# The state's products moved from behind the scores to ahead of the outputs, as two tiles instead of four

## What is computed

```python
A = jnp.einsum('bhntd,bhnsd->bhnts', q, k)
A = A * jnp.where(mask, jnp.exp(jnp.where(mask, dec, 0.0)), 0.0)
o_intra = jnp.einsum('bhnts,bhnsd->bhntd', A, v)
...
o_int = jnp.einsum('bhtd,bhde->bhte', qc * jnp.exp(gcc)[..., None], S)
kd = kc * jnp.exp(gtc[..., None] - gcc)[..., None]
S = jnp.exp(gtc)[..., None, None] * S + jnp.einsum('bhtd,bhte->bhde', kd, vc)
```

## Time and profile before

| | us |
|---|---|
| median of 3 runs | 402.62 (401.43 to 403.20) |
| the profiled execution | 398.42 |
| its span, first to last instruction | 396.7 |
| PE busy | 372.7 (94%) |
| DVE busy | 306.7 (77%) |
| ACT busy | 289.2 (73%) |
| POOL busy | 279.7 (71%) |

### The profile page before, as it was taken

How to read it: one execution, slowest core, us unless ns; L and a number is a source line. 1 busy time by engine, 2 the same in 40 slices (tenths; PEclk the granted TensorE clock), 3 DMA queues, 4 the chain that set the end, 5 groups by cost and what they waited for, 6 DMA issues and landing times.

```text
span 396.7 us, 14345 instructions
## 1 busy us (share of the span) xinstructions
PE 372.7 (94%) x4077; PEld 318.2 (80%) x4078; DVE 306.7 (77%) x859; ACT 289.2 (73%) x889; POOL 279.7 (71%) x245
## 2 busy tenths in 40 slices
PE   7997799999999999999999998999999999999990
PEld 6665577777777787787787877899999999999990
DVE  4988798999888889888888889567767767677750
ACT  3888887888788887878787885566667666666660
POOL 8002553687788877888788863388888888888883
PEclk9996999999999999999999999999999999999996
DMA  8944579457465545566564522254545455455530
GB/s 232 247 136 151 198 244 325 138 169 193 158 202 148 152 132 161 162 197 179 167 190 118 167 65 67 44 70 65 72 64 68 62 70 68 59 74 67 61 32 0
DMA packets 59097, 51.31 MB, mean 129 GB/s; under 512 B 7200, under 2 KB 51392, under 8 KB 59072
## 3 DMA queue, kind: packets, MB, share of 16 engines
q1 hardware_dynamic: 45936, 42.07, 37.6%
q0 software_dynamic: 12272, 8.54, 15.4%
q10 hardware_dynamic: 864, 0.40, 0.4%
HBM read 33.14 MB, written 18.30 MB: 130 GB/s over the span
## 4 chain that ended last, share of the span: by engine, by line
PE 63%; ACT 13%; DVE 9%; issue 7%; DMA 3%; POOL 2%; ACTq 1%; DVEq 1%; SPq 0%; POOLq 0%
PE psA L977 16%; PE psVG L965 16%; PE psVG L771 11%; PE psT L859 7%; ACT sq L1157 3%; DVE ms L1470 3%; ACT v_sb L1139 3%; ACT E L1148 3%; ACT th L1130 2%; PE psO L825 2%; PE psKS L814 2%; DMA x_all<-in_L_attn_x_dram 2%; DVE kd L1514 2%; PE psA L648 1%; PE psKS L956 1%
## 5 line engine op out<-in xcount | busy, mean ns | idle before, releaser
L620 POOL DMA_INDIRECT out_dram<-yw,sidx x71 | 114.8, 1618 | 29.4 <-DVE yw L1685 9.0
L1148 ACT ACTIVATE E<-gcB,ngc 128x128 f32<-128x128 f32 x256 | 78.4, 404 | 0.9 <-DMA gcB<-decay_rows 0.9
L577 POOL DMA_INDIRECT sorted_rows<-x_all,pos_i x64 | 63.8, 998 | 13.5 <-issue 9.2
L561 POOL TENSOR_TENSOR rms<-msn,neg_half 128x8 f32<-128x8 f32 x32 | 54.3, 1697 | 24.2 <-DVE msn L1474 23.8
L554 POOL TENSOR_SCALAR_AFFINE_SELECT E<-E 128x1024 f32<-128x1024 f32 x32 | 35.1, 1095 | 42.9 <-ACT E L1148 30.8
L1130 ACT ACTIVATE th<-psVG,x_all 128x256 f32<-128x256 f32 x64 | 26.8, 470 | 31.7 <-PE psVG L771 31.7
L825 PEld LDWEIGHTS psO<-v_sb,pr 128*64 128x64 f32 x1024 | 33.3, 141 | 13.8 <-issue 13.5
L825 PE MATMUL psO<-v_sb,pr 128*64 128x64 f32 x1024 | 37.7, 228 | 3.0 <-DVE pr L1503 3.0
L977 PE MATMUL psA<-xT_all,v_sb 128*128 x288 | 38.4, 277 | 0.4 <-DVE yb L1683 0.4
L965 PE MATMUL psVG<-xgT,gcB 128*128 128x128 f32 x288 | 38.6, 278 | 0.0
L977 PE MATMUL psA<-xT_all,th 128*128 x280 | 37.9, 279 | 0.5 <-issue 0.2
(11 more groups left out here) (210 smaller groups left out, 948.0 us busy)
## 6 DMA issues: line engine op xcount, KB each, us to landing
gcB<-decay_rows SPq DMA_DIRECT2D x32, 512.0 KB, 4.9
sorted_rows<-blank SPq DMA_DIRECT2D x12, 396.0 KB, 5.7
xg<-sorted_rows SPq DMA_DIRECT2D x71, 66.0 KB
x_all<-in_L_attn_x_dram SPq DMA_DIRECT2D x16, 256.0 KB, 5.2
out_dram<-res SPq DMA_DIRECT2D x32, 128.0 KB, 2.0
eqB<-decay_exp_rows SPq DMA_DIRECT2D x32, 64.0 KB
w1b<-in_L_ffn_w_dram SPq DMA_DIRECT2D x8, 256.0 KB
xT_all<-in_L_ffn_w_dram SPq DMA_DIRECT2D x32, 64.0 KB
```

Source lines behind the costliest of these rows:

```text
L561: nc.gpsimd.tensor_tensor(rms[:], msn[:], neg_half[:, 0:2 * H], ALU.pow).then_inc(rms_ready, 1)
L577: nc.gpsimd.indirect_dma_start(out=sorted_dram, out_offset=bass.IndirectOffsetOnAxis(ap=pos_i[:, t:t + 1], axis=0), in_=x_all[:, t, :], in ...
L620: nc.gpsimd.indirect_dma_start(out=out_rows, out_offset=bass.IndirectOffsetOnAxis(ap=sidx[j][:], axis=0), in_=yw[j][:], in_offset=None, bo ...
L1148: last = nc.scalar.activation(E[j][:, k, h * P:(h + 1) * P], gcB[j][:, k * H + h, :], ACT.Exp, bias=ngcf[:, bass.ds((s * 2 + k) * H + h, 1)])
```

## The change

`state` makes two products instead of four: for each pair of heads all 64 key columns by the 128 value columns of both heads. So it computes the blocks of head a's keys by head b's values as well; the copy's mask, which now takes 128 columns of psKS twice instead of 64 four times, sets them to zero as it did with the repeated ones. Each product is a tile of 64 output partitions, as in the outputs. In `step` the call moves from behind `scores` to behind `proj_vg`, directly ahead of `outputs`. The waits of `state` (kd_ready, v_copied) move with it. The calls outside `step` (sequences 0, 1 and 31) keep their place and take the new form.

```diff
                 pe.wait_ge(kd_ready, s + 1)
                 pe.wait_ge(v_copied, s + 1)
-                for h in range(H):
-                    last = nc.tensor.matmul(psKS[h * DK:(h + 1) * DK, HV:HV + DV], kd[:, h * DK:(h + 1) * DK], v_sb[j][:, 0, h * DV:(h + 1) * DV],
-                                            start=True, stop=True)
+                for c in range(2):
+                    last = nc.tensor.matmul(psKS[c * 2 * DK:(c + 1) * 2 * DK, HV:HV + 2 * DV], kd[:, c * 2 * DK:(c + 1) * 2 * DK],
+                                            v_sb[j][:, 0, c * 2 * DV:(c + 1) * 2 * DV], start=True, stop=True)
                 last.then_inc(s_ready, 1)
...
                 first_keys(i, j)
                 proj_qk(*turn(i, j, 1, 2))
                 scores(i, j)
-                state(i, j)
                 project_out(*turn(i, j, -2, 2))
                 if extra:
                     extra()
                 proj_vg(*turn(i, j, 1, 2))
                 if behind_vg:
                     behind_vg()
+                state(i, j)
                 outputs(i, j)
                 transpose_on(*turn(i, j, -1, 2))
...
-                nc.vector.tensor_tensor(S_sb[:].rearrange("p (h d) -> p h d", d=DV), bc(psKS[:, HV:HV + DV].unsqueeze(1), [P, H, DV]),
-                                        headmask[:].rearrange("p (h d) -> p h d", d=DV), ALU.mult).then_inc(s_copied, 1)
+                nc.vector.tensor_tensor(S_sb[:].rearrange("p (c n) -> p c n", c=2), bc(psKS[:, HV:HV + 2 * DV].unsqueeze(1), [P, 2, 2 * DV]),
+                                        headmask[:].rearrange("p (c n) -> p c n", c=2), ALU.mult).then_inc(s_copied, 1)
```

## The result

The changed kernel takes 403.0 us in the median of 21 runs (401.7 to 405.3), the kernel before 401.4 in 21 runs beside it (399.5 to 403.6): a ratio of 1.0036, 95% interval 1.0022 to 1.005, which is 0.9 to 2.0 us; the medians differ by 1.6. The change is slower by less than the 0.5% that the prediction took as its line. The forecast, 404.7, stands 1.7 too high, and its own range, 403.4 to 406.0, begins 0.4 above the measured time: 1.2 of the 1.7 is the base (402.6 was the median of three runs, 401.4 that of 21), 0.5 the sum (+2.1 for +1.6).

The account below looks back on a forecast made before the run. A ring from outputs through square, sum, kd, state, project_out and proj_vg bounds the lap. 0.22 inserted less 0.15 slack gives +0.07 over 20 laps, plus 0.7 elsewhere: +2.1 on 402.6, so 404.7 us, range 403.4 to 406.0.

Parts of the forecast that it names:

- The ring through square, sum and kd: Outputs, square, sum, kd, state, project_out, proj_vg, outputs: this ring sets the lap at 6.45, against PE's own 6.32.
- The state's new form, +0.22: State's two rounds of 0.11, ahead of the outputs, lengthen the ring by 0.22; bounds 0.11 to 0.44.
- the first rival: PE's own order bounds the lap, with one mode-change drain gone: laps of 6.29, 399.2 us; chance 0.12.
- The slack at proj_vg, 0.15: proj_vg, released by the probabilities, can come 0.15 earlier, not 0.38: lag 0.23 now, 0.08 then.
- Laps of 6.44 and 6.45: Lap lengths of the attention loop in the earlier trace, forecast to become 6.52, +0.07 each.
- The steps outside: Steps outside the 20 laps from 98 to 227 us: step 2 gains 0.3, others lose, together +0.7 us.
- The sum: Whole kernel: 20 laps of 0.07 plus 0.7 for the other steps, +2.1 us.
- PE's order as the bound: Square or probabilities have slack, so PE's own length sets laps of 6.29: 399.2 us; chance 0.12.
- Cheap state: State's rounds cost only 0.11 in the new place, laps 0.04 shorter: 401.9 us; chance 0.12.
- Late copy: DVE's state copy ends over 0.25 later than put, or the mode drains once more: 407.4 us; chance 0.09.
- Serial tiles: State's two tiles run one after the other, insertion 0.44, 0.22 more per step: 410.6 us; chance 0.05.

Follow-up runs that it names:

- form: Kernel before with the new two 64-column state products at the old place behind the scores: 402.8 us, ratio 1.0056 to the kernel before.
- after_look1: The changed kernel, unchanged, in a third traced execution: span 403.9 us.
- before_kd_first: Kernel before with DVE's kd (decay_k) put ahead of the sum of squares: 406.2 us, ratio 1.012 to the kernel before.
- place: Changed kernel with the old four 32-column state products at the new place ahead of the outputs: 407.6 us, ratio 1.0151 to the kernel before.
- before_two: Kernel before with two scatters in every step and the 14 left all in step 29: 414.1 us, ratio 1.0267 to the kernel before.
- after_two: Changed kernel with two scatters in every step and the 14 left all in step 29: 415.5 us, ratio 1.0295 to the kernel before.
- before_gap: Kernel before with a GpSimd fill between the two back-to-back scatters of three-scatter steps: 407.1 us, ratio 1.0097 to the kernel before.
- after_gap: Changed kernel with a GpSimd fill between the two back-to-back scatters of three-scatter steps: 406.5 us, ratio 1.0084 to the kernel before.

## Why the prediction came out as it did

*What bounds a lap.* Right for undisturbed laps. The ring through square, sum and kd is shown by form, and in the changed kernel it closes through the probabilities: PE's waits name them, and no wait for kd is left.

*The state's new form, +0.22.* Right to the hundredth between state and outputs. From proj_vg to the outputs' end it is 3.40 (131.81 to 135.21) for 3.16: +0.24, since the state starts 0.02 later behind proj_vg than the own halves did.

The step on which the first rival rested was the drain at a change of tiling. The last score is 0.21 ahead of project_out in the changed kernel (130.53 to 130.74), as it was ahead of the state in the earlier trace rows; behind proj_vg one change is left as before, and state and own halves, of one tiling, have none between them. From the state to what follows it is 0.27 in the same tiling (own halves, changed kernel) and 0.37 across a change of it (project_out, form): 0.10 for the change, if nothing else sets the two apart, which no run tells. That PE time was saved, and it didn't count, as PE's own length is not the bound. By the Trainium skill (TensorEngine Tiling (Array Packing), Key Properties) PE drains on a change of the mode and not of the tile alone; the two figures agree with that.

*The slack at proj_vg, 0.15.* This is the step of the prediction that failed: the mechanism was right, and the term was mis-sized. It was 0.23 - 0.08: a mean of 0.21 and 0.25, read from sums of rounded rows (0.22 and 0.25 unrounded in that trace), less a lag to which I had added the time from the load to its product. Measured, from the pair with two scatters a step: proj_vg starts 0.25 and 0.26 behind the probabilities in the old kernel's two kinds of lap, and 0.055 behind them in both of the changed one. Slack 0.20. The probabilities also end 0.01 to 0.02 sooner behind the outputs, since the square takes 0.60 where it took 0.61 to 0.62. 0.235 - 0.20 - 0.02 = +0.017, as the laps say. 20 x 0.07 = 1.4 should have been 20 x 0.017 = 0.3.

*Laps of 6.44 and 6.45.* Here the prediction rested on a row that was true and not typical. In the other traces half of the laps are 6.73 to 6.82, in both kernels, and in these the change costs nothing that can be seen, as the scatters set them. In the four typical traces before and three after, proj_vg 11 to 31 is 132.7 (132.5 to 133.1) and 133.1 (133.0 to 133.4): +0.4, of which 0.15 is the last lap.

*The steps outside.* Step 2 gained 0.3 as forecast (lap 2 is 8.32 for 8.64). Laps 3 to 5 lose 0.13, 0.14 and 0.24, forecast +0.5. Laps 6 to 8 were to lose 0.1 and lose 0.56, all of it in lap 7, which holds the first late signal: 7.64 for 6.85 to 7.25 before. With two scatters a step lap 7 is 6.59 for 6.61, so it is how the disturbance falls, not the change's own length. Lap 9 loses 0.0 for 0.1. From proj_vg 2 to 11 that is +0.76 in the typical traces (64.3 to 65.1), +0.27 in the pair of two. The forecast's own sum for these steps doesn't fit its text: it has a term of 0.2 where the text gives 3 x 0.03 for steps 6 to 8, and with the text's terms it is +0.6, not +0.7.

*The sum.* From step 2 on the typical traces give 0.76 + 0.42 - 0.29 (behind proj_vg 31) = +0.9, where +1.6 (0.9 to 2.0) is measured; without after_look1, whose part behind proj_vg 31 is 0.65 shorter than in the other two, it is +1.2. The forecast had +1.4 for the loop, where the loop gave 0.3 by the undisturbed laps, and +0.7 for the rest, where lap 7 alone took 0.56 that belongs to the disturbance. So the sum, 0.5 off, is as near as that by luck: a loop term more than four times too large stood in for a loss that the prediction didn't know of. The remaining 0.4 to 0.7 can't be placed: the time until step 2 differs by 5 us between executions of one kernel, and seven traces don't tell its mean to 0.5. The pair of two differs by 1.4 in its times and by 1.7 in its traces' spans: 0.8 from proj_vg 2 to 31 (of which 0.19 is the lap with the stall of step 29), 0.8 behind proj_vg 31, which stays open.

*The rivals.* PE's order as the bound: refuted, PE waits for the probabilities in every lap (0.055 behind them). Cheap state: refuted, it adds 0.22. Late copy: refuted, it ends 0.29 ahead of the outputs' second part, which starts 0.93 behind the first. Serial tiles: refuted by the same 0.22, for which they would need 0.44.

*Open.* Why the scatters delay TensorE, whether it takes two of them in a row, and why one traced execution of the kernel before, of five, showed nothing of it with its scatters at the same place, no run tells. Whether it is the fetch of PE's instructions that suffers wasn't tried.

## What to carry to other kernels

When an instruction leaves a wait, look for the next resource that its successor waits for: here 0.38 of PE time left a place and 0.20 of it could be used. When a step is put ahead of another on a queue, ask what it waits for itself, as kd showed. And take a second trace of the kernel before: a base whose laps are all alike in one execution had every second one 0.3 to 0.37 longer in the next four, and a change of 0.02 a lap can't be read against that without taking the disturbance out of both.

## What the runs showed of the hardware

- In steps with three scatters on GpSimd, two of them directly behind each other (0.96 to 1.03 each, 0.30 between them), a TensorE signal comes 0.23 to 0.46 late, 0.55 to 1.02 in the first such steps and about 0.9 beside the scores, and from step 10 on 0.66 to 0.83 behind the end of the second scatter (0.80 to 1.14 late and 0.67 to 0.95 behind it in before_kd_first); or a product starts 0.4 to 0.7 late (place). With two scatters in every step, the mask of 1.1 between them, no signal is late (before_two and after_two, all laps of the loop). In the kernel before it costs 4.7 us from proj_vg 2 to 31: 192.3 in the undisturbed trace, 197.0 in the mean of the other four.
- A fill of 0.45 and its wait, which put 1.27 between the two scatters, don't end it but move it: the scores' signals are 0.34 to 0.47 late (before_gap) and up to 1.18 (after_gap).
- The state as two 64-column tiles of 128 moving columns adds 0.22 inside a stretch of that tiling and takes 0.37 between others; as four 32-column tiles of 64 it takes 0.25 in both places.
- A start of PE behind the end of the DVE instruction that releases it takes 0.055 in the loop (proj_vg in the changed kernel).
